# Graph layers on one core: products two steps behind the transposes, and five buffers for widened blocks

## The chip, the cores and the metric

The kernel runs on one core of a Trainium2 chip. The time is that of one launch on the device, in microseconds; the median of three runs counts.

## What is computed

Four graph blocks over 6250 nodes with 256 features, each followed by a residual and a normalisation. The second of them is three layers of one kind, so six times the kernel sums rows of neighbours over 106250 edges and multiplies the sums with 256x256 matrices:

```python
x_neigh = segment_sum(edge_w[:, None] * x[src], dst, N)         # pass 0
out = x @ w_self.T + x_neigh @ w_neigh.T                        # then row norm, residual, layernorm

z = (1.0 + eps) * h + segment_sum(h[src], dst, N)               # passes 1, 2, 3
m = relu(z @ W1 + b1) @ W2 + b2
h = relu(layernorm(m + h) * gamma + beta)

x = segment_sum(h * rsqrt(deg_out))[...] * rsqrt(deg_in) @ W_gc + feats @ W_res     # pass 4
core = top-2 of 64 experts (256 -> 512 -> 256)                  # between passes 4 and 5

out = (x - segment_sum(edge_val * x[col]) * (diag + 1)) @ weight + bias             # pass 5
```

## The kernel before, in words

The 6250 rows are 49 tiles of 128. A pass makes, tile by tile, the sum over edges in PSUM on PE, then the matrix products, the normalisation and the new rows, which go to HBM for the next pass. A tile's sum comes in one of three ways. **Sparse** tiles: POOL gathers the source rows of 128 edges with one indirect DMA (L2394), DVE makes a one-hot of their targets (picks, L3077 and L3079), PE multiplies the two (L2469, L2473, L2476); 18 such chunks make a tile. **Dense** tiles (24 of 49, in passes 1 to 4): the adjacency counts of the tile against all 49 source tiles lie in HBM as blocks of bytes, built once in pass 0; SP loads them in parts of seven blocks (`AB`, four buffers), ACT widens them to 32 bits in parts of three or four blocks (`widen`, L2944, into `WIDE`), and PE multiplies a block with the resident rows of its source tile (L2498 in passes 2 to 4, L2501 in pass 1). **Weighted** tiles (8 in pass 0, 13 in pass 5): blocks with edge weights are made on the fly from one-hots (L2523, L2563 on PE, L2909 and L2911 on ACT, L3198 on DVE).

The order is written out by hand in **steps**. A step has three gathered chunks; passes 0 to 5 have 246, 150, 150, 150, 150 and 216 such steps and a few more in which the last tiles run out (`STEPS`). In every pass each engine runs a loop over the same steps and does its own share of each, so a step is no barrier: each engine waits only for the semaphores that its instructions need. About 8.3 dense blocks belong to a step of passes 1 to 4. `SEQ` gives the step in which a tile's sum is complete: 6j+5 for sparse tiles, steps 1 and 3 of six for dense ones (so all are odd, often two apart), 2 of six for weighted ones (three from a sparse neighbour). The table `OFFSETS` says how many steps later each event of the tile is done:

- Z: the operand is made of the sum (DVE L3344, L3347, L3350; ACT L2821 in pass 0).
- T: PE transposes it into PSUM bank 2 (L2601), ACT copies it out to `TZT` (L2831).
- H (passes 1 to 3): PE multiplies with W1 (L2610), ACT takes bias and relu into `TM1` (L2838).
- L: PE makes the layer's product (L2625), from `TM1` in passes 1 to 3, from `TZT` in the others.
- A, F, Q, F2, Q2, F3, N, R: norm, residual and statistics (DVE L3376, L3378), root on ACT (L2813), scaling, new rows, their low parts. S: SP stores them. GT, G, LG: the gate of the experts in pass 4 (PE L2634, L2652 and the ranks L2642 to L2644; ACT L2861; DVE L3420 and on).
- O and X: SP loads rows for pass 4 and pass 3.

On PE a step is: dense blocks, three chunks, then the events in the order of the tiles, then building work of passes 0 and 5. On ACT it is: the widening for the next step's blocks, copies of built blocks, events, one-hots. A part of blocks is widened one step ahead of its use:

```python
return k, max(0, dense_step(b) - 1)                    # L1435, the step at which a part is widened
if e >= XA:
    act.wait_ge(s_dq, e - XA + 1)                      # in widen: part e-XA is done with
```

DVE's step is: picks for two steps ahead (which wait for the chunks of the step before, since the ring has four groups), the events, then background work: sorting edges into bins (L3082 on), one-hots of blocks (L3198), histograms (L3263 to L3266). The transposes wait for the copy of the transposes before; in passes 0 and 5, whose layer product lies in the same PSUM bank, they also wait for the finish (F) of the tile before:

```python
if k in (0, 5) and n or k == 1 and p == 0:
    pe.wait_ge(s_u, n)                                 # in transposes
```

In the eight steps after a pass's last chunk PE also multiplies the first 28 blocks of the next pass (`HEAD_PACE` = 4, 1, 1, 1, 1, 6, 7, 7 by step). The next pass's gathers wait for all new rows to be stored.

Of the kernel before, what the change touches and what calls it, by code (L numbers as in the profile page):

```python
# [5 lines left out]
N = 6250  # L6
# [34 lines left out]
def general(nc, ctx, a, out, PS):  # L41
# [1322 lines left out]
GT = WT // GC  # L1364
# [34 lines left out]
AW = max(b - a for a, b in zip(QB, QB[1:])) * P // 4  # L1399
XB = sorted({b for a, e in zip(QB, QB[1:]) for b in (a, (a + e + 1) // 2)} | {NT})  # L1400
XN = len(XB) - 1
XA = 3
XW = max(b - a for a, b in zip(XB, XB[1:])) * P
RP = 2 * D
HST = RP + 2
# [8 lines left out]
MCR = 120  # L1414
PACK_AT = [1 + 25 * i // 8 for i in range(len(SPARSE[5]))]
LASTB = {0: 26, 5: 7 + PACE}
OFFSETS = [dict(Z=1, T=2, L=3, A=4, F=5, Q=6, F2=7, N=8, R=9, S=10)] + \
    [dict(O=-1, Z=1, T=2, H=3, L=4, F=5, Q=6, F2=7, R=8, S=9)] * 2 + \
    [dict(O=-1, Z=1, T=2, H=3, L=4, X=4, F=5, Q=6, F2=7, Q2=8, F3=9, N=9, R=10, S=11)] + \
    [dict(O=-1, Z=1, T=2, L=3, F=4, GT=5, G=6, LG=7), dict(Z=1, T=2, L=3, F=4, Q=5, F2=6, N=7)]  # L1420
STEPS = [GROUPS[k] + max(9, *OFFSETS[k].values()) for k in range(PASSES)]


# [41 lines left out]
for _k in range(PASSES):  # L1465
    for _p, (_e, _t, _, _) in enumerate(SEQ[_k]):
        for _name, _o in OFFSETS[_k].items():
            EVENTS[_k].setdefault(_e + _o, []).append((_name, _p))
# [10 lines left out]
for _k in range(1, 5):  # L1479
    _at = 0  # L1480
    for _r in range(RBG):
        _stored = max(SEQ[_k - 1][PLACE[_k - 1][t]][0] for t in range(3 * _r, min(3 * _r + 3, NT))) + OFFSETS[_k - 1]["S"]
        _at = max(_at + 1, _stored + 2, (GROUPS[0] - 6 if _k == 1 else DSTEPS + 1) + _r)
# [21 lines left out]
def gnn(nc, a, out):  # L1505
# [5 lines left out]
    with ctx:  # L1511
# [40 lines left out]
        WIDE_AT = -(-PL // 8) * 8  # L1552
        BB = -(-(WIDE_AT + XA * XW) // 8) * 8
        PLANES = rounded("plane_rows", 0, PL)
        WIDE = rounded("wide_blocks", WIDE_AT, XA * XW)
        SLOTR = rounded("slot_rows", 3 * NT * D, RING * GC * HST)
# [470 lines left out]
        def events(k, g):  # L2027
            return sorted(EVENTS[k].get(g, []), key=lambda e: (e[1], OFFSETS[k][e[0]]))

# [410 lines left out]
        def _(pe):  # L2440
# [38 lines left out]
            def dense(k, found):  # L2479
                for b in found:  # L2480
# [8 lines left out]
                    if i == 0 and t % 3 == 0:  # L2489
# [5 lines left out]
                        pe.wait_ge(s_rl[r % 3], 16 * (r // 3 + 1))  # L2495
                    at_block = e % XA * XW + (t - XB[x]) * P
                    if k > 1:
# [296 lines left out]
        def _(act):  # L2794
# [139 lines left out]
            def widen(k, e):  # L2934
# [4 lines left out]
                if XB[x] == QB[q]:  # L2939
                    act.wait_ge(s_al[n % QA], 16 * (n // QA + 1))  # L2940
                if e >= XA:
                    act.wait_ge(s_dq, e - XA + 1)
                lo, w = (XB[x] - QB[q]) * P, (XB[x + 1] - XB[x]) * P
                fn(WIDE[:, e % XA * XW:e % XA * XW + w], AB[n % QA][:, lo:lo + w], ACT.Copy).then_inc(s_ax, 1)  # L2944

# [745 lines left out]
```

## Time and profile before

| | us |
|---|---|
| three runs | 5908.39, 5938.55, 5950.65 |
| median | 5938.55 |
| profiled execution | 5919.13 |
| its span, first to last instruction | 5917.4 |

Over the span PE is busy 4715.8 us (80%), DVE 3840.7 (65%), POOL 3409.4 (58%), ACT 2329.9 (39%), and TensorE's granted clock is 0.905 of full on average. By the transposes, passes 0 to 4 begin at 75, 1215, 1931, 2675 and 3382 us, pass 5 at 4982; between passes 4 and 5 lie the experts. Busy times are unions of an engine's instructions; the idle time in a row of lines is that of the engine just before the instructions of the row, with what ended it. "remote" is a semaphore whose setter the profile cannot name, "issue" no release that it shows.

### The profile page before, as it was taken

To read this page: it belongs to the slowest core of one execution; us is meant where nothing else is said; L and a number is where in the kernel's file an instruction comes from. 1 tells how busy PE (TensorE), PEld (TensorE's weight loads), DVE (VectorE), ACT (ScalarE), POOL (GpSimd) and SP (SyncE) were. 2 spreads that over 40 slices of the span, in tenths; PEclk is the share of its full clock that TensorE was granted. 3 is DMA by queue.
4 is the path that set the end of the run, shared out by engine and by line. 5 is a ranking of instruction groups with operands and counts; after the bars stand their busy time and mean duration, and the time that the engine had idled before them with its cause. 6 is when DMAs were issued, how large, how long until landed. Compare 5 with 4: busy or idle time off the path is not lost.

```text
span 5917.4 us, 84727 instructions
## 1 busy us (share of the span) xinstructions
PE 4715.8 (80%) x26215; PEld 3890.9 (66%) x26215; DVE 3840.7 (65%) x12470; ACT 2329.9 (39%) x5927; POOL 3409.4 (58%) x3425
## 2 busy tenths in 40 slices
PE   5988976678886777868888688884989857889896
PEld 3877764478885666656666477663878734777775
DVE  6788888367776777647889454447777545444443
ACT  3888875333332333324444233330333213333332
POOL 5666666566665555656666566552433263666665
PEclk8999998789998999989999799886999968999998
DMA  5333334577778666787778877663999933333333
GB/s 147 109 116 112 119 115 122 188 225 217 218 221 284 199 204 198 219 288 229 244 241 247 297 219 219 202 205 115 318 308 318 303 86 100 97 96 97 97 98 88
DMA packets 598239, 1113.22 MB, mean 188 GB/s; under 512 B 107962, under 2 KB 347320, under 8 KB 597500
## 3 DMA queue, kind: packets, MB, share of 16 engines
q0 software_dynamic: 221664, 684.44, 39.8%
q1 hardware_dynamic: 376122, 423.29, 21.8%
q8 instruction: 218, 3.57, 0.2%
q14 instruction: 235, 1.93, 0.1%
HBM read 994.01 MB, written 114.65 MB: 187 GB/s over the span
## 4 chain that ended last, share of the span: by engine, by line
PE 38%; another core or an unknown queue 9%; issue 9%; DVE 6%; ACT 2%; POOL 2%; DMA 2%; SPq 0%; ACTq 0%; DVEq 0%; POOLq 0%
PE PS L2498 11%; PE PS L2730 4%; PE PS L2625 4%; PE PS L2739 3%; PE PS L2469 3%; PE PS L2563 3%; PE PS L2476 3%; PE PS L2523 2%; POOL ring L2394 1%; PE PS L2610 1%; PE PS L2749 1%; ACT wide_blocks L2944 1%; PE PS L2601 1%; POOL ring L2423 1%
## 5 line engine op out<-in xcount | busy, mean ns | idle before, releaser
L2394 POOL DMA_INDIRECT slot_rows<-planes,REC x1800 | 1741.2, 967 | 1075.7 <-issue 468.4
L2944 ACT ACTIVATE wide_blocks<-HH 128x512 fp32r<-128x512 uint8 x1344 | 741.2, 573 | 1074.2 <-PE PS L2498 467.4
L2498 PE MATMUL PS<-plane_rows,wide_blocks 128*128 128x512 f32 x3528 | 1028.1, 434 | 122.0 <-ACT wide_blocks L2944 82.4
L2498 PEld LDWEIGHTS PS<-plane_rows,wide_blocks 128*128 128x128 f32 x3528 | 691.1, 204 | 300.4 <-ACT wide_blocks L2944 98.9
L2394 POOL DMA_INDIRECT ring<-in_x,REC x555 | 539.2, 971 | 312.9 <-issue 143.0
L2394 POOL DMA_INDIRECT ring<-table,REC x486 | 467.9, 963 | 319.1 <-issue 208.9
L2476 PE MATMUL PS<-ring,pick 128*128 128x256 f32 x2082 | 565.5, 408 | 81.6 <-DMA ring<-in_x,REC 26.9
L2476 PEld LDWEIGHTS PS<-ring,pick 128*128 128x128 f32 x2082 | 409.5, 204 | 169.7 <-issue 48.2
L2523 PE MATMUL PS<-HH 128*128 128x256 f32 (+2 forms) x1650 | 396.3, 357 | 150.4 <-issue 56.0
L2563 PE MATMUL PS<-HH 128*128 128x256 f32 x2058 | 504.3, 387 | 10.4 <-issue 10.2
L3079 DVE TENSOR_SCALAR slot_picks<-iotab,REC 128x128 fp32r<-128x128 bf16 x1800 | 411.7, 301 | 96.0 <-remote 43.9
L2909 ACT ACTIVATE HH<-iota,HH 128x128 bf16<-128x128 f32 (+1 forms) x962 | 329.3, 392 | 342.9 <-remote 197.1
L2414 POOL DMA_INDIRECT ring<-second_outputs,ring x120 | 222.2, 1852 | 411.6 <-PE PS L2720 326.8
L2469 PE MATMUL PS<-slot_rows,slot_picks 128*128 128x512 f32 x1350 | 424.6, 423 | 34.5 <-DMA slot_rows<-planes,REC 25.1
L2563 PEld LDWEIGHTS PS<-HH 128*128 128x128 f32 x2058 | 396.3, 195 | 72.7 <-issue 17.1
L2501 PE MATMUL PS<-plane_rows,wide_blocks 128*128 128x256 f32 (+1 forms) x2352 | 356.8, 303 | 78.7 <-ACT wide_blocks L2944 42.2
L2625 PE MATMUL PS<-WA,TZT 128*128 128x256 f32 x980 | 289.7, 443 | 148.8 <-ACT TZT L2831 124.5
L2523 PEld LDWEIGHTS PS<-HH 128*128 128x128 f32 (+1 forms) x1650 | 254.9, 164 | 231.6 <-issue 162.1
L2831 ACT ACTIVATE TZT<-PS 128x256 f32<-128x256 f32 (+1 forms) x294 | 132.5, 451 | 662.1 <-remote 442.7
L2501 PEld LDWEIGHTS PS<-plane_rows,wide_blocks 128*128 128x128 f32 x2352 | 318.0, 202 | 95.5 <-issue 44.3
L3077 DVE TENSOR_SCALAR pick<-iotab,REC 128x128 f32<-128x128 bf16 x1041 | 300.2, 359 | 121.2 <-remote 38.2
L3200 DVE TENSOR_SCALAR HH<-HH 128x256 f32<-128x256 f32 x338 | 127.2, 419 | 381.9 <-remote 218.7
(376 smaller groups left out, 8911.7 us busy)
## 6 DMA issues: line engine op xcount, KB each, us to landing
HH<-in_L_gnn_w SPq DMA_DIRECT2D x240, 512.0 KB
HH<-dense_blocks SPq DMA_DIRECT2D x672, 112.0 KB
plane_rows<-planes SPq DMA_DIRECT2D x64, 768.0 KB
planes<-HN SPq DMA_DIRECT2D x188, 256.0 KB
slot_rows<-planes,REC POOLq DMA_INDIRECT x1800
dense_blocks<-HH SPq DMA_DIRECT2D x24, 784.0 KB
more<-in_L_gnn_b SPq DMA_DIRECT2D x120, 128.0 KB
expert_outputs<-ring SPq DMA_DIRECT2D x120, 128.0 KB
```

Source lines behind the costliest of these rows:

```text
L2394: pool.indirect_dma_start(to, None, planes[k] if dense else tables[k], bass.IndirectOffsetOnAxis(ap=at_rows, axis=0)).then_inc(s_slot[slot ...
L2469: last = mm(bank(j % 2, RP), slot_pick(k, slot), slot_row(k, slot, 0, RP), start=c == 0, stop=c == WT - 1)
L2476: last = mm(bank(j % 2, D), slot_pick(k, slot), slot_row(k, slot, 0, D), start=c == 0, stop=c == WT - 1)
L2498: last = mm(bank(5 + n % 2, RP), WIDE[:, at_block:at_block + P], plane(0, t, RP), start=t == 0, stop=t == NT - 1)
L2501: last = mm(bank(5 + n % 2, w), WIDE[:, at_block:at_block + P], plane(m, t, w), start=t == 0 and m == 0, stop=t == NT - 1 and m == 1, skip ...
L2523: last = mm(bank(b, w, j * 2 * P), sources[slot][:, j * P:(j + 1) * P], targets[slot][:, j * 2 * P:j * 2 * P + w], start=True, stop=not ow ...
L2563: last = mm(bank(sums_bank(v), D), AW32[f % OWN][:, s % 4 * P:(s % 4 + 1) * P], x_tile(SUMMED[v][0], s), start=pos == 0 and s == sources[0 ...
L2625: last = mm(bank(layer_bank(k), D), v, wmat(m, b), start=i == 0, stop=i == len(pairs) - 1)
L2909: last = fn(to[:, j * P:(j + 1) * P], iota[:, :], ACT.Square, bias=lanes[:, 1, 2 * m + j:2 * m + j + 1], scale=-1.0)
L2944: fn(WIDE[:, e % XA * XW:e % XA * XW + w], AB[n % QA][:, lo:lo + w], ACT.Copy).then_inc(s_ax, 1)
L3077: last = v.tensor_scalar(p, iotab, lo, we, ALU.is_equal, ALU.mult)
L3079: last = v.tensor_scalar(p, iotab, lo, None, ALU.is_equal)
```

## The change

`XA`, the number of buffers for widened parts, becomes 5 (it takes 1024 more words of each partition's row, and what lies behind moves up). In `OFFSETS` H stands two steps after T in place of one, and L two steps after H (passes 1 to 3) or after T (passes 0, 4, 5) in place of one; all later events move by as much, 1 or 2 steps, and in pass 4 the gate's product is one step further behind its transposes. The extra steps at a pass's end grow by one or two.

```diff
-XA = 3
+XA = 5
...
-OFFSETS = [dict(Z=1, T=2, L=3, A=4, F=5, Q=6, F2=7, N=8, R=9, S=10)] + \
-    [dict(O=-1, Z=1, T=2, H=3, L=4, F=5, Q=6, F2=7, R=8, S=9)] * 2 + \
-    [dict(O=-1, Z=1, T=2, H=3, L=4, X=4, F=5, Q=6, F2=7, Q2=8, F3=9, N=9, R=10, S=11)] + \
-    [dict(O=-1, Z=1, T=2, L=3, F=4, GT=5, G=6, LG=7), dict(Z=1, T=2, L=3, F=4, Q=5, F2=6, N=7)]
+OFFSETS = [dict(Z=1, T=2, L=4, A=5, F=6, Q=7, F2=8, N=9, R=10, S=11)] + \
+    [dict(O=-1, Z=1, T=2, H=4, L=6, F=7, Q=8, F2=9, R=10, S=11)] * 2 + \
+    [dict(O=-1, Z=1, T=2, H=4, L=6, X=6, F=7, Q=8, F2=9, Q2=10, F3=11, N=11, R=12, S=13)] + \
+    [dict(O=-1, Z=1, T=2, L=4, F=5, GT=6, G=8, LG=9), dict(Z=1, T=2, L=4, F=5, Q=6, F2=7, N=8)]
```

PE in the middle of pass 2, before. L2601 are a tile's transposes, L2610 and L2625 its two products, L2498 dense blocks, L2469 chunks, L2580 a histogram:

```order
L2625 MATMUL PS<-WA,TM 128x256 x2
L2601 MATMUL PS<-ident,TZ 128x128 x2
L2498 MATMUL PS<-plane_rows,wide_blocks 128x512 x9
L2469 MATMUL PS<-slot_rows,slot_picks 128x512 x3
L2610 MATMUL PS<-TZT,WA 128x128 x4
L2498 MATMUL PS<-plane_rows,wide_blocks 128x512 x8
L2469 MATMUL PS<-slot_rows,slot_picks 128x512 x3
L2580 MATMUL PS<-HH 128x49 x18
L2625 MATMUL PS<-WA,TM 128x256 x2
```

and after, from a tile's transposes to its first product (its second product is the next L2625, six rows further on):

```order
L2601 MATMUL PS<-ident,TZ 128x128 x2
L2498 MATMUL PS<-plane_rows,wide_blocks 128x512 x9
L2469 MATMUL PS<-slot_rows,slot_picks 128x512 x3
L2498 MATMUL PS<-plane_rows,wide_blocks 128x512 x8
L2469 MATMUL PS<-slot_rows,slot_picks 128x512 x3
L2580 MATMUL PS<-HH 128x49 x18
L2625 MATMUL PS<-WA,TM 128x256 x2
L2610 MATMUL PS<-TZT,WA 128x128 x4
```

A tile's first product stood one step of blocks and chunks behind its transposes. Now two steps lie between, and the first product shares its step with the second product of the tile before.

ACT at the same place, before. L2831 copies transposes, L2838 is the relu, L2944 widens, L2813 is a root:

```order
L2838 ACTIVATE TM<-PS,B1C 128x128 x2
L2944 ACTIVATE wide_blocks<-HH 128x512
L2944 ACTIVATE wide_blocks<-HH 128x384
L2831 ACTIVATE TZT<-PS 128x256
L2944 ACTIVATE wide_blocks<-HH 128x512
L2944 ACTIVATE wide_blocks<-HH 128x384
L2944 ACTIVATE wide_blocks<-HH 128x512
L2838 ACTIVATE TM<-PS,B1C 128x128 x2
L2944 ACTIVATE wide_blocks<-HH 128x384
```

and after:

```order
L2838 ACTIVATE TM<-PS,B1C 128x128 x2
L2831 ACTIVATE TZT<-PS 128x256
L2944 ACTIVATE wide_blocks<-HH 128x512
L2944 ACTIVATE wide_blocks<-HH 128x384
L2944 ACTIVATE wide_blocks<-HH 128x512
L2944 ACTIVATE wide_blocks<-HH 128x384
L2944 ACTIVATE wide_blocks<-HH 128x512
L2838 ACTIVATE TM<-PS,B1C 128x128 x2
L2944 ACTIVATE wide_blocks<-HH 128x384
```

The relu now stands just ahead of the next copy of transposes. The widening stands behind the copy as before.

DVE in pass 0, at the sixth tile, whose follower is a weighted tile, before. L3374 to L3322 are the tile's finish, L3077 picks, L3138 and L3140 sorting, L3198 one-hots:

```order
L3077 TENSOR_SCALAR pick<-iotab,REC 128x128 x3
L3374 TENSOR_SCALAR SM<-SM 128x1
L3375 RECIPROCAL SM<-SM 128x1
L3376 SCALAR_TENSOR_TENSOR TU<-PS,SM,HH 128x256
L3320 BN_STATS ST<-TU 128x6
L3321 BN_AGGR MV<-ST 128x2
L3322 TENSOR_SCALAR SM<-MV 128x1
L3138 TENSOR_TENSOR HH<-LANES,PS 128x2304
L3198 TENSOR_SCALAR HH<-HH 128x256 x4
L3077 TENSOR_SCALAR more<-iotab,REC 128x128 x3
L3140 CAST PS<-HH 128x90
L3141 TENSOR_TENSOR HH<-iotab,PS 128x468
```

and after:

```order
L3077 TENSOR_SCALAR pick<-iotab,REC 128x128 x3
L3138 TENSOR_TENSOR HH<-LANES,PS 128x2304
L3198 TENSOR_SCALAR HH<-HH 128x256 x4
L3077 TENSOR_SCALAR more<-iotab,REC 128x128 x3
L3374 TENSOR_SCALAR SM<-SM 128x1
L3375 RECIPROCAL SM<-SM 128x1
L3376 SCALAR_TENSOR_TENSOR TU<-PS,SM,HH 128x256
L3320 BN_STATS ST<-TU 128x6
L3321 BN_AGGR MV<-ST 128x2
L3322 TENSOR_SCALAR SM<-MV 128x1
L3140 CAST PS<-HH 128x90
L3141 TENSOR_TENSOR HH<-iotab,PS 128x468
```

The finish has moved behind L3138, the one-hots and the picks of the step after.

## Rows read from the trace of the kernel before

**Rows 1.** Stretches of passes 0 to 4: us, busy of PE, PEld, DVE, ACT, POOL; PEclk; DMA.

```profile
60.00:1170.00 1110.00, 890.18 (x4436) 716.36 (x4437) 847.58 (x2876) 776.95 (x2106) 694.93 (x714) 0.91 0.40 122
1170.00:1885.00 715.00, 581.22 (x4178) 548.02 (x4178) 513.29 (x1620) 237.43 (x582) 441.85 (x452) 0.90 0.77 235
1885.00:2628.00 743.00, 572.27 (x3197) 444.33 (x3196) 492.64 (x1284) 231.29 (x532) 430.92 (x452) 0.91 0.73 220
2628.00:3330.00 702.00, 559.37 (x2554) 432.78 (x2553) 563.36 (x1810) 292.06 (x726) 443.62 (x451) 0.91 0.81 253
3330.00:4090.00 760.00, 600.88 (x2655) 478.95 (x2654) 376.15 (x1622) 230.71 (x439) 428.88 (x452) 0.87 0.69 206
```

**Rows 2.** Lines of POOL, whole span: POOL's gathers of passes 1 to 4.

```profile
L2394 POOL DMA_INDIRECT slot_rows<-planes,REC x1800 | 1741.2, 967 | 1075.7 <-issue 468.4 <-remote 293.9 <-PE PS L2469 248.9
```

**Rows 3.** Lines of PE, pass 1: busy us, mean ns | idle before us, releasers.

```profile
L2501 PE MATMUL PS<-plane_rows,wide_blocks 128*128 128x256 f32 (+1 forms) x2334 | 353.8, 303 | 78.7 <-ACT wide_blocks L2944 42.2 <-issue 29.8 <-DVE plane_rows L3463 5.4
L2625 PE MATMUL PS<-WA,TM 128*128 128x256 f32 x192 | 57.3, 426 | 24.3 <-ACT TM L2838 13.8 <-issue 10.4
```

**Rows 4.** Lines of PE, pass 2.

```profile
L2498 PE MATMUL PS<-plane_rows,wide_blocks 128*128 128x512 f32 x1176 | 340.7, 434 | 27.1 <-ACT wide_blocks L2944 21.6 <-issue 5.5
L2625 PE MATMUL PS<-WA,TM 128*128 128x256 f32 x196 | 60.8, 437 | 20.8 <-issue 16.9 <-ACT TM L2838 4.0
L2610 PE MATMUL PS<-TZT,WA 128*128 128x128 f32 x395 | 57.5, 291 | 35.7 <-ACT TZT L2831 31.3 <-issue 4.3
```

**Rows 5.** Lines of PE, pass 3.

```profile
L2498 PE MATMUL PS<-plane_rows,wide_blocks 128*128 128x512 f32 x1176 | 341.4, 430 | 54.4 <-ACT wide_blocks L2944 36.6 <-issue 17.5
L2625 PE MATMUL PS<-WA,TM 128*128 128x256 f32 x196 | 59.0, 428 | 32.5 <-ACT TM L2838 23.2 <-issue 9.2
```

**Rows 6.** Lines of PE, pass 4.

```profile
L2498 PE MATMUL PS<-plane_rows,wide_blocks 128*128 128x512 f32 x1170 | 342.9, 437 | 40.5 <-ACT wide_blocks L2944 24.2 <-issue 16.1
L2625 PE MATMUL PS<-WA,TZT 128*128 128x256 f32 x392 | 122.6, 468 | 72.5 <-ACT TZT L2831 72.3 <-issue 0.2
```

**Rows 7.** Waits of ACT: total us, times, longest us.

```profile
ACT wide_blocks L2944 <- PE PS L2498: 467.4, 354, 7.1
ACT TZT L2831 <- remote: 442.7, 85, 18.7
```

**Rows 8.** Timeline, pass 4: start us, us, engine, line [idle before <-releaser].

```profile
3755.57 0.42 PE L2601 MATMUL PS<-ident,TZ 128*128 128x128 f32 x2
...
3763.51 0.62 DVE L3420 TENSOR_TENSOR HH<-HH,PS 128x64 f32<-128x64 bf16 x4 [7.25 <-remote]
3763.57 0.60 ACT L2831 ACTIVATE TZT<-PS 128x512 f32<-128x512 f32 x1 [8.85 <-remote]
...
3764.22 3.78 PE L2625 MATMUL PS<-WA,TZT 128*128 128x256 f32 x8 [5.44 <-ACT TZT L2831]
```

**Rows 9.** Timeline, end of pass 2, PE alone.

```profile
2629.28 1.13 PE L2625 MATMUL PS<-WA,TM 128*128 128x256 f32 x4 [0.48 <-ACT TM L2838]
2630.06 6.88 PE L2498 MATMUL PS<-plane_rows,wide_blocks 128*128 128x512 f32 x28
```

**Rows 10.** Pass 0: PE's line of the product, then a timeline of one place.

```profile
L2625 PE MATMUL PS<-WA,TZT 128*128 128x256 f32 x392 | 106.4, 420 | 22.8 <-ACT TZT L2831 11.4 <-issue 11.3
...
308.06 0.48 DVE L3376 SCALAR_TENSOR_TENSOR TU<-PS,SM,HH 128x256 f32<-128x256 f32 x1
...
308.69 0.41 PE L2601 MATMUL PS<-ident,TZ 128*128 128x128 f32 x2 [0.65 <-issue]
...
309.33 2.54 DVE L3138 TENSOR_TENSOR HH<-LANES,PS 128x2304 bf16<-128x2304 bf16 x1
...
311.79 0.87 DVE L3198 TENSOR_SCALAR HH<-HH 128x256 bf16<-128x256 bf16 x4
...
312.57 0.85 DVE L3077 TENSOR_SCALAR pick<-iotab,REC 128x128 f32<-128x128 bf16 x3
```

**Rows 11.** Lines of PE, pass 5.

```profile
L2625 PE MATMUL PS<-WA,TZT 128*128 128x256 f32 x196 | 60.7, 438 | 53.5 <-ACT TZT L2831 40.7 <-issue 12.8
```


## The prediction

> **What bounds the kernel now.** I read the stretches first. Passes 1 to 4 take 715, 743, 702 and 760 us. No engine is full in any of them: PE has 559 to 601 us busy, DVE 376 to 563, ACT 231 to 292, POOL 429 to 444 [rows 1]. POOL adds 468.4 us of its own spacing between 1800 gathers to 1741.2 us of work [rows 2], so it needs about 552 us of a pass. The passes are bound by waits between engines that all run in a fixed order.
>
> The second view is the PE's lines of each pass with the idle time ahead of them. Ahead of the products over widened blocks (L2498, L2501) PE idles 78.7, 27.1, 54.4 and 40.5 us, mostly until ACT has widened a block: 200.7 us [rows 3 to 6]. Ahead of the second product on the relu'd operand (L2625 on TM) it idles 24.3, 20.8 and 32.5 us, together 77.6; ahead of the first product (L2610) 35.7 in pass 2, where it matters; ahead of pass 4's product on transposes (L2625 on TZT) 72.5 [rows 3 to 6]. These 386 us are copies on ACT that come too late.
>
> The third view, the waits, says why ACT is late with blocks: its widening waits 467.4 us, in 354 places, for PE to give a buffer of the three back, and its copy of transposes waits 442.7 us for a signal [rows 7]. The timeline of one place in pass 4 shows the second kind: the transposes start at 3755.57, PE goes on with a step of 11 products until 3758.8, ACT's copy starts only at 3763.57, and PE sits 5.44 us until 3764.22. DVE, which waits for the gate's products just ahead of those transposes, is let go at the same moment, after 7.25 us [rows 8]. PE's matmuls are drawn as ended long before ACT is let go. So a signal of PE can be 7 us late, and what counts is how much work PE has that needs nothing behind that signal.
>
> The Trainium skill (Perfetto Trace Analysis, "Summary: the profiler window per engine type") says that a matmul's end in a profile is estimated and the signal's way is not in it; the trace agrees, and shows far more than a propagation here.
>
> **Part one, five buffers.** A part of 3 or 4 blocks is widened one step before it is used, and today waits for the part three before it; with five, for the part five before it. PE has then four parts, 14 blocks or 1.7 steps of some 4.5 us, between the signal and the need, in place of two parts. Such lateness as rows 8 show is 7 us at worst, so waits of this kind should nearly all go. Not all of the 200.7 us is of this kind: part has no releaser in the view. I take 0.7 of it, 140 us. The bounds are 0 and 200.7.
>
> **Part two, products two steps behind.** The first product moves from one to two steps after the transposes, the second from one to two steps after the first, and every later event by as much. One thing does not move: ACT's copy of the transposes, and behind it, on ACT, the widening for the step after next. The order of ACT shows blocks queued right behind the copies. So where a late signal of the transposes holds ACT, PE runs one step, skips what was the first product, and stops at the next block instead. The 35.7 us ahead of L2610 I therefore count as not gained (bounds: 35.7 gained; 20 lost, since ACT has relu, copy and a widening, 1.6 us, ahead of PE's next work where it had one copy).
>
> The wait for the relu is another matter. Tiles end on odd steps alone; first product and transposes now share odd steps, and even steps hold neither. ACT has one place per two steps to be held in place of two. I take half of 77.6 us, 39 us (bounds 0 and 77.6). In pass 4 the product, 122.6 us in 49 tiles or 2.5 us each [rows 6], now stands between the gate's small products and the transposes, and the signal that is late is that of the gate's products: the transposes' share of the lateness shrinks by that. Half of 72.5 us, 36 us (bounds 0 and 72.5).
>
> The Trainium skill (TensorE: Matmul & The Clock Gate, "Architectural detail: the array is 16× 32×32, not 1× 128×128") has ACT and DVE as strict first-in first-out queues. That rule speaks against this part. Taken alone it would give part two nothing in the passes with blocks; rival one below is that case.
>
> Together 215 us of PE's waits. What comes late next: DVE (563 us busy of 702 in pass 3, with its chained small steps between) and POOL's 552 us and the idle time between passes. I keep 0.55 of it, a choice between 0 and 1 nearer the middle because no engine is busy for more than 81% of any of these passes [rows 1]: 118 us.
>
> **Where it costs.** At the end of passes 0 to 3 the last tile's products stand among the 28 blocks with which the next pass begins: the first now has one block more before it, the second seven more. 28 blocks take 6.88 us, so 0.246 each: eight are 2.0 us, less waits of PE that they fill, such as the 0.48 us ahead of the product now [rows 9]. Some 1 us at each of four ends: 4 us.
>
> Pass 0: transposes and the layer's product share a PSUM bank, so the next tile's transposes wait for DVE's finishing of this one. A weighted tile ends 3 steps from its neighbours. There the transposes already follow DVE's finish by 0.15 us (308.06 with 0.48 us, then 308.69). Now DVE's finish stands behind one more piece of the background work: 2.54 us, 0.87 us and the next picks 0.85 us, 4.3 us later [rows 10]. Eight such places are 34 us of PE, the eight other neighbours about 1 us each. DVE, with 848 of 1110 us busy [rows 1], sets the pace there and mostly does not wait for PE, so I count 15 us (bounds 0 and 42). Ahead of the product itself 22.8 us of waits may shrink [rows 10]; that is inside this 15.
>
> Pass 5 has the same rule and 26 such places, but no sorting on DVE. PE waits 53.5 us ahead of L2625 [rows 11]. Builds behind the same ACT queue take over half of it, and the later finish some 17 us: a gain of 10 us (bounds 40 gained, 30 lost).
>
> **Sum.** -118 +4 +15 -10 = -109 us. The profiled execution took 5919.1 us (span 5917.4), so 5810; the median of three is 5938.55, 19 us above it, and a change is compared in medians: 5830.
>
> **Rivals.**
> One: the stall only moves. ACT is held by the same late signals, and PE stops at the next block. For it: rows 8, and that ACT's order is unchanged. Against: 467.4 us of ACT's wait is for buffers. Then part one keeps 40 us and the rest cancels against 19 us of costs: 5915.
>
> Two: the full release. The waits go and nothing takes their place; all 215 us come through, with the same 9 us of costs: 5733. For it: POOL's 552 us. Against: DVE's load in passes 1 to 3.
>
> Three: slower. The finish that comes a DVE step later turns passes 0 and 5 into a hand-over in every weighted neighbourhood: the transposes wait, ACT's copies and one-hots queue behind them, and DVE then lacks its inputs. The price is a DVE step, 4.3 us, at all 16 + 26 places, 180 us, less 110 us in the blocks' passes: 6010. It decides when PE, behind at such a place, also starves DVE's picks two steps on; PE is at 890 of 1110 us in pass 0, so it isn't far. Against: DVE has as much work left in the step as PE has to catch up.
>
> Four: that the change doesn't do what it says. The order shows it does, on all three engines.
>
> **Chances.** Forecast 0.49 (its own range 5770 to 5885), rival one 0.21, rival two 0.15, rival three 0.15. The range 5740 to 5960 takes in most of rivals one and two and leaves rival three out. A measurement of this kernel can tell about 1% (59 us) from no change. Faster by over 1%: nearly all of the forecast and all of rival two, 0.62. Within 1%: rival one and the forecast's upper edge, 0.23. Slower: 0.15.
>
> **What would show it.** ACT's wait for PE L2498 ahead of its widening should fall from 467.4 us to under 200, and PE's idle time ahead of the blocks from 200.7 to about 60 to 100. The waits ahead of L2625 on TM should halve; those ahead of L2610 should vanish from that line, with blocks in their place just after odd steps. Passes 1 to 4 should each lose 15 to 40 us. In pass 0, PE's idle time ahead of L2601 at the weighted neighbourhoods should rise from 0.65 us in rows 10 to some 4. I am wrong if the idle time ahead of the blocks doesn't fall, or if passes 0 or 5 grow by over 30 us.

## The result

| eleven runs each, side by side | median, us | lowest to highest |
|---|---|---|
| before | 5942.17 | 5908.39 to 5952.92 |
| changed | 5960.73 | 5952.2 to 5972.2 |

The ratio is 1.0036, with a 95% interval of 1.0019 to 1.0053: the change costs 0.4%. The forecast was 5830 us, and the time lies 0.7 us above the range of 5740 to 5960; it moved the other way than forecast. The two profiled executions took 5919.13 and 5952.2 us (spans 5917.4 and 5950.5), 33 us apart. Measured from a pass's first transposes to its last, the lengths are:

| us | pass 0 | 1 | 2 | 3 | 4 | 5 | the rest of the span |
|---|---|---|---|---|---|---|---|
| before | 1091.7 | 668.9 | 696.3 | 653.7 | 700.6 | 921.6 | 1184.6 |
| changed | 1135.1 | 667.7 | 711.7 | 656.1 | 666.2 | 924.4 | 1189.3 |
| difference | +43.4 | -1.2 | +15.3 | +2.4 | -34.4 | +2.8 | +4.7 |

So pass 0 lost 43 us, and passes 1 to 4, where 118 us were to be gained, gained 18: pass 4 alone gained 34, and passes 1 to 3 together lost 17. Each of these lengths is from one execution of each kernel. The changed kernel's stretches between those transposes, passes 0 to 4, with the columns of [rows 1]:

```profile
75.19:1210.28 1135.09, 881.25 (x4384) 713.29 (x4382) 836.72 (x2836) 776.55 (x2098) 685.61 (x705) 0.90 0.39 117
1258.55:1926.24 667.69, 561.95 (x4002) 525.94 (x4001) 496.08 (x1555) 215.71 (x557) 419.11 (x427) 0.91 0.76 229
1972.76:2684.44 711.68, 558.06 (x3081) 435.98 (x3077) 478.55 (x1243) 199.98 (x505) 409.42 (x427) 0.89 0.71 215
2731.00:3387.14 656.14, 536.18 (x2451) 423.24 (x2450) 546.16 (x1747) 265.70 (x694) 415.24 (x427) 0.90 0.80 250
3440.39:4106.55 666.16, 548.43 (x2539) 442.01 (x2538) 351.37 (x1515) 199.53 (x407) 405.67 (x428) 0.91 0.72 215
```

The waits that the change was to cure did go from where they stood. PE's lines of passes 1 to 4, in this order, in stretches that answer to those of [rows 3 to 6]:

```profile
L2501 PE MATMUL PS<-plane_rows,wide_blocks 128*128 128x256 f32 (+1 forms) x2332 | 354.8, 302 | 74.8 <-issue 53.8 <-ACT wide_blocks L2944 14.4 <-DVE plane_rows L3463 5.6
L2625 PE MATMUL PS<-WA,TM 128*128 128x256 f32 x192 | 57.3, 425 | 0.9 <-issue 0.8
...
L2498 PE MATMUL PS<-plane_rows,wide_blocks 128*128 128x512 f32 x1177 | 340.2, 432 | 82.9 <-ACT wide_blocks L2944 74.5 <-issue 8.4
L2610 PE MATMUL PS<-TZT,WA 128*128 128x128 f32 x397 | 61.3, 304 | 1.9 <-ACT TZT L2831 1.9
...
L2498 PE MATMUL PS<-plane_rows,wide_blocks 128*128 128x512 f32 x1176 | 341.5, 431 | 65.1 <-ACT wide_blocks L2944 34.7 <-issue 29.8
L2625 PE MATMUL PS<-WA,TM 128*128 128x256 f32 x196 | 55.1, 406 | 7.6 <-ACT TM L2838 6.0 <-issue 1.7
...
L2498 PE MATMUL PS<-plane_rows,wide_blocks 128*128 128x512 f32 x1169 | 335.8, 429 | 89.3 <-ACT wide_blocks L2944 50.8 <-issue 38.5
L2625 PE MATMUL PS<-WA,TZT 128*128 128x256 f32 x392 | 101.5, 405 | 0.7 <-ACT TZT L2831 0.7
```

The second product (L2625) waited 77.6 us in three passes and 72.5 in pass 4; now it waits 11 and 0.7. But ahead of the blocks (L2501, L2498) PE idles 312 us where it had been 200.7. The waits of ACT tell why, beside [rows 7]; the row of DVE is pass 0's and is taken up further down. First the relu's wait in the kernel before, then the changed kernel's rows:

```profile
ACT TM L2838 <- remote: 139.9, 27, 12.1
```

```profile
ACT TM L2838 <- remote: 551.4, 85, 16.0
ACT TZT L2831 <- remote: 412.7, 77, 22.8
...
DVE SM L3374 <- ACT SM L2809: 138.9, 31, 11.8
...
ACT wide_blocks L2944 <- PE PS L2498: 170.5, 114, 6.7
```

The widening waits much less for a buffer (170.5 us by this row, 467.4 before); it now stands behind the relu and the copy, which wait for a signal of PE. Taking all rows of a line together, whatever they name, ACT's waits ahead of the widening fell from 1068 to 456 us, those ahead of the relu rose from 210 to 724 and those ahead of the copy of transposes from 661 to 751: 612 us went, 604 came. A place in pass 2, in the changed kernel's timeline:

```profile
2492.78 2.11 PE L2498 MATMUL PS<-plane_rows,wide_blocks 128*128 128x512 f32 x8
...
2494.73 0.86 PE L2469 MATMUL PS<-slot_rows,slot_picks 128*128 128x512 f32 x3
...
2501.39 0.62 ACT L2838 ACTIVATE TM<-PS,B1C 128x128 f32<-128x128 f32 x2 [12.91 <-remote]
...
2501.91 1.97 ACT L2944 ACTIVATE wide_blocks<-HH 128x384 fp32r<-128x384 uint8 x4
...
2502.48 1.22 PE L2498 MATMUL PS<-plane_rows,wide_blocks 128*128 128x512 f32 x2 [6.90 <-ACT wide_blocks L2944]
```

PE's first product is over by 2493.0, it goes on through eight blocks and three chunks, and then waits 6.90 us for a block. ACT widens that block straight after the relu, and the relu had been waiting 12.91 us, the last 8.4 of them after the product was drawn as ended. It is the picture of [rows 8], with the block in the product's place. (Whether the block's bytes and buffer were there much earlier than the relu, the trace doesn't show; when ACT reached it they were.)

### The profile page after: what moved, and what is told of

It is laid out like the page before. It is cut to its first block, busy times and chain, and to the rows that moved or that the text cites. A ratio compares the mean times of both kernels' runs of the same rounds, so it can differ in the third digit from the quotient of the medians.

```text
span 5950.5 us, 84745 instructions
## 1 busy us (share of the span) xinstructions
PE 4745.3 (80%) x26215; PEld 3920.6 (66%) x26215; DVE 3846.3 (65%) x12470; ACT 2277.2 (38%) x5927; POOL 3399.4 (57%) x3425
## 3 DMA queue, kind: packets, MB, share of 16 engines
q1 hardware_dynamic: 376122, 423.29, 21.5%
## 4 chain that ended last, share of the span: by engine, by line
PE 34%; DVE 10%; issue 9%; another core or an unknown queue 8%; DMA 2%; ACT 2%; POOL 1%; SPq 0%; ACTq 0%; DVEq 0%; POOLq 0%
PE PS L2498 8%; PE PS L2563 4%; PE PS L2730 4%; PE PS L2739 4%; PE PS L2476 3%; PE PS L2625 3%; PE PS L2469 3%; PE PS L2523 2%; DVE slot_picks L3079 1%; ACT wide_blocks L2944 1%; PE PS L2749 1%; PE PS L2601 1%; POOL ring L2423 1%; DVE HH L3266 1%
## 5 line engine op out<-in xcount | busy, mean ns | idle before, releaser
L2498 PE MATMUL PS<-plane_rows,wide_blocks 128*128 128x512 f32 x3528 | 1020.7, 431 | 237.3 <-ACT wide_blocks L2944 160.0
L2498 PEld LDWEIGHTS PS<-plane_rows,wide_blocks 128*128 128x128 f32 x3528 | 696.5, 205 | 432.6 <-ACT wide_blocks L2944 182.5
L2944 ACT ACTIVATE wide_blocks<-HH 128x512 fp32r<-128x512 uint8 x1344 | 690.0, 571 | 457.1 <-PE PS L2498 170.5
L2469 PE MATMUL PS<-slot_rows,slot_picks 128*128 128x512 f32 x1350 | 436.3, 430 | 66.3 <-DMA slot_rows<-planes,REC 42.8
L2831 ACT ACTIVATE TZT<-PS 128x256 f32<-128x256 f32 (+1 forms) x294 | 133.8, 455 | 752.9 <-remote 412.7
L2501 PE MATMUL PS<-plane_rows,wide_blocks 128*128 128x256 f32 (+1 forms) x2352 | 357.9, 302 | 74.8 <-issue 53.8
L2501 PEld LDWEIGHTS PS<-plane_rows,wide_blocks 128*128 128x128 f32 x2352 | 322.3, 205 | 90.5 <-issue 68.8
L2469 PEld LDWEIGHTS PS<-slot_rows,slot_picks 128*128 128x128 f32 x1350 | 276.9, 206 | 153.3 <-issue 61.9
L2838 ACT ACTIVATE TM<-PS,B1C 128x128 f32<-128x128 f32 x294 | 92.0, 364 | 724.2 <-remote 551.4
```

What stands on the lines that cost most here:

```text
L2469: last = mm(bank(j % 2, RP), slot_pick(k, slot), slot_row(k, slot, 0, RP), start=c == 0, stop=c == WT - 1)
L2498: last = mm(bank(5 + n % 2, RP), WIDE[:, at_block:at_block + P], plane(0, t, RP), start=t == 0, stop=t == NT - 1)
L2501: last = mm(bank(5 + n % 2, w), WIDE[:, at_block:at_block + P], plane(m, t, w), start=t == 0 and m == 0, stop=t == NT - 1 and m == 1, skip ...
```

## Two kinds of chip

The runs below fell on two kinds of chip, which nothing in the program chooses. On most, the kernel before takes 5237 to 5246 us, 12% less than in the runs above. The thirteenth and fourteenth run were on one like the first, at 5875 us. Ratios are always to the kernel before on the same chip. Each chip was used at one time only, so whether the kind belongs to the chip or to a state it was in is not shown; "kind of chip" below means no more than that.

The fifth run is the kernel before itself on the faster chip.

> The kernel before, for a profile of it on the chip that took 5243 us for it. Theory 'prompt signals' (this chip lets ACT and DVE go as soon as PE's matmuls are drawn as ended, the chip of the prediction did not): PE's idle time in passes 1 to 4 is some 280 us against 596 us in rows 3 to 6's execution, and hardly any signal of PE comes over 2 us after its matmul's recorded end. Rival 'clock': the idle time is as in the first profile, and the 700 us lie in fewer stretches at half clock.

Measured: 5236.93 us. Its stretches of passes 0, 2 and 4 and its waits of ACT:

```profile
76.14:1070.05 993.91, 844.66 (x4384) 687.82 (x4382) 827.53 (x2838) 772.85 (x2099) 692.00 (x705) 0.95 0.44 134
...
1715.43:2286.88 571.45, 511.83 (x3080) 405.58 (x3076) 476.77 (x1245) 228.59 (x505) 410.12 (x430) 0.96 0.85 266
...
2988.63:3546.55 557.92, 517.16 (x2539) 419.93 (x2538) 352.37 (x1531) 222.35 (x407) 406.63 (x427) 0.97 0.83 257
```

```profile
ACT wide_blocks L2944 <- PE PS L2498: 527.9, 737, 12.8
ACT TZT L2831 <- PE PS L2601: 519.4, 243, 12.2
...
PE PS L2498 <- ACT wide_blocks L2944: 12.9, 4, 5.1
...
PE PS L2625 <- ACT TZT L2831: 4.6, 11, 0.7
```

ACT's waits for PE now name it ("remote" is gone), and PE waits 12.9 us for ACT's blocks of passes 2 to 4, where it had waited 82.4. ACT itself still waits long, 714 us ahead of the widening against 1068 and 519 ahead of the copy against 661, but this costs PE little. Of the recorded updates of the semaphore that PE's transposes raise, 105 of 251 in the first profile come over 2 us after the recorded end of the transposes before them, and here one of 295, the last of the trace. (Six passes of 49 tiles raise it 294 times; in the first profile some of these have no record of their own.) DVE, ACT and POOL are as fast on the one as on the other (POOL's work in pass 2 is 406 and 410 us). So the first chip's signals of PE are late, and this one's are prompt. Whether a late signal is slow on its way or its matmul ends later than it is drawn, the trace can't tell apart; what follows needs only that the waiting engine is let go late. In passes 1 to 4 PE's idle time is 247 us here, against 537 there, both between transposes; PE's busy time is smaller too (pass 2: 512 against 542 us), at a granted clock of 0.96 against 0.92. The expectation held for the signals and the idle time; its rival has a share: of the 419 us by which passes 1 to 4 are shorter here, 290 are PE's idle time and 129 its busy time.

## The change in parts, on a chip with prompt signals

The buffers alone:

```diff
-XA = 3
+XA = 5
```

> Five buffers, every offset as before. Theory 'moved' (ACT is held by late signals of PE, and PE stops at whatever it needs from ACT next): ACT's wait for PE L2498 ahead of the widening falls from 467 us to under 200, but PE's idle time moves to L2610, L2625 and to blocks behind the relu and the copy of transposes; the idle time of passes 1 to 4 together falls by 20 to 50 us of 596, the time is 5900 to 5930. Rival 'buffers cure, offsets spoil': the 165 us of idle time that ended with a buffer given back are gained, passes 1 to 4 are 100 to 150 us shorter, 5790 to 5840. Rival 'clock': the idle time falls but the granted clock falls with it, and the time stays within 5 us of 5942.

Measured: 5233.15 us, ratio 0.9976 (0.9967 to 0.9985): 10 us. On this kind of chip PE hardly waits for blocks, so there was little to move or to cure, and the expectation, made for the other kind, stays untested.

The offsets alone (all of `OFFSETS` new, `XA = 3`):

> All new offsets, three buffers as before. Theory 'moved': the waits for the relu and the copy go from L2625 and L2610, the waits for buffers stay at L2498 and L2501 (some 165 us or more), pass 0 has its whole loss of 43 us: 5970 to 6010. Rival 'offsets help': the copies' waits of 180 us fall to half, and with pass 0's loss the time is 5900 to 5930.

Measured: 5342.62 us, ratio 1.0188 (1.0175 to 1.0201). Pass 0 takes 1072.4 us, against 993.9 in the fifth run; no other pass is over 16 us longer. The ratio is above that of the whole change on this kind of chip (1.0136, below), clear of both intervals: beside the new offsets the five buffers are worth 0.5%, by themselves 0.2%. What the 0.5% are made of was not looked at.

The change in passes 1 to 4 alone:

```diff
-OFFSETS = [dict(Z=1, T=2, L=4, A=5, F=6, Q=7, F2=8, N=9, R=10, S=11)] + \
+OFFSETS = [dict(Z=1, T=2, L=3, A=4, F=5, Q=6, F2=7, N=8, R=9, S=10)] + \
...
-dict(Z=1, T=2, L=4, F=5, Q=6, F2=7, N=8)]
+dict(Z=1, T=2, L=3, F=4, Q=5, F2=6, N=7)]
```

> The changed kernel, with the offsets of before in passes 0 and 5. Theory 'finish' (the 43 us that pass 0 lost come of its own offsets): pass 0 is back at 1092 us between its first and last transposes, passes 1 to 4 stay as in the changed kernel, 5910 to 5925. Rival (pass 0's loss is a chance of one execution, or comes from the head of pass 1 and its buffers): pass 0 keeps 20 us or more of the loss, and the time stays above 5940.

Measured: 5244.41 us, ratio 1.0003 (0.9994 to 1.0011), with pass 0 at 999.5 us. The whole change on such a chip:

> The changed kernel beside the experiments, on their chip if it is to be had. Theory 'finish': its passes 0 and 5 are those of the second experiment (pass 0 75 us longer than before), its passes 1 to 4 those of the third (no change): 1.013 to 1.016 times before. Rival: the five buffers take part of pass 0's loss away, since the first 28 blocks of pass 1 are widened at its end: under 1.008. On a chip with late signals of PE, as that of the prediction, 1.0036 as before.

Measured: 5318.43 us, ratio 1.0136 (1.0121 to 1.0152). Pass 0 is 77 us longer than before, pass 5 3 us shorter, and passes 1 to 4 together level (+4.7, +11.2, -9.8, -5.5). On this kind of chip the loss is pass 0's. ACT's waits move here as they did on the first chip (ahead of the widening 714 to 209 us, of the relu 162 to 548, of the copy 519 to 657), but here ACT is back in time: PE idles 13 us ahead of the blocks of passes 1 to 4, against 15 in the kernel before. (The expectation's rival, that the buffers take part of pass 0's loss away, fails: it is 77 us with them and 78 without.)

## Why pass 0 lost

First the fifth run's timeline (before), then the sixth's (changed), at the same weighted tile:

```profile
368.86 0.48 DVE L3376 SCALAR_TENSOR_TENSOR TU<-PS,SM,HH 128x256 f32<-128x256 f32 x1
...
369.50 0.41 PE L2601 MATMUL PS<-ident,TZ 128*128 128x128 f32 x2 [2.87 <-DVE TU L3376]
...
374.24 1.89 PE L2625 MATMUL PS<-WA,TZT 128*128 128x256 f32 x8
...
379.23 0.20 ACT L2809 ACTIVATE SM<-SM 128x1 f32<-128x1 f32 x1
...
380.47 0.15 DVE L3374 TENSOR_SCALAR SM<-SM 128x1 f32<-128x1 f32 x1
```

```profile
393.66 0.48 DVE L3376 SCALAR_TENSOR_TENSOR TU<-PS,SM,HH 128x256 f32<-128x256 f32 x1
...
394.29 0.66 PE L2601 MATMUL PS<-ident,TZ 128*128 128x128 f32 x2 [9.73 <-DVE TU L3376]
...
404.92 1.89 PE L2625 MATMUL PS<-WA,TZT 128*128 128x256 f32 x8
...
410.20 0.20 ACT L2809 ACTIVATE SM<-SM 128x1 f32<-128x1 f32 x1
...
410.54 0.15 DVE L3374 TENSOR_SCALAR SM<-SM 128x1 f32<-128x1 f32 x1 [4.55 <-ACT SM L2809]
```

Finish, transposes, product, root and finish are a loop through all three engines, since transposes and product share a bank. Two things happen in it. The transposes wait 9.73 us for the finish in place of 2.87: DVE does it a step later. And from the transposes to the product it is now 10.6 us in place of 4.7, so the root comes late, and DVE, which had not waited at this place, stands still for 4.55. The first wait stands in nine places of pass 0, which has eight weighted tiles, the second in 29 (rows below). Two runs take them apart. The seventh leaves the product late and puts the finish back:

```diff
-OFFSETS = [dict(Z=1, T=2, L=4, A=5, F=6, Q=7, F2=8, N=9, R=10, S=11)] + \
+OFFSETS = [dict(Z=1, T=2, L=4, A=5, F=5, Q=7, F2=8, N=9, R=10, S=11)] + \
```

> The changed kernel with one number changed: in pass 0 DVE's finish F stands five steps after the sum, as before, though the product L stays two steps behind the transposes. Theory 'finish' (what pass 0 lost is that PE's transposes of a weighted neighbour wait for a finish that DVE does a step later than PE does the transposes): pass 0 is within 12 us of that of before and the time is 60 us or more under the changed kernel's. Rival 'product' (the loss is L's own move, which fills the step of the neighbour's transposes): nothing is gained, pass 0 stays 40 to 75 us longer than before.

Measured: 5298.01 us, ratio 1.0106 (1.0089 to 1.0123), pass 0 1050.4 us: 20 us under the changed kernel. Neither side was right: the finish is neither the whole loss nor nothing. The seventh is not a clean half of the change, though: the root (A) is late with the product, and the finish that needs it (F) now stands in the same step, where both kernels have a step between. The eighth is the third experiment's kernel with the finish late and product and root as before:

```diff
-OFFSETS = [dict(Z=1, T=2, L=3, A=4, F=5, Q=6, F2=7, N=8, R=9, S=10)] + \
+OFFSETS = [dict(Z=1, T=2, L=3, A=4, F=6, Q=7, F2=8, N=9, R=10, S=11)] + \
```

> The third experiment's kernel, with pass 0's product L and root of the norm where they were, and DVE's finish F and all behind it one step later, as the change has them. Theory 'finish': the whole loss of pass 0 is there (70 to 80 us where PE's signals are prompt, 40 to 50 where they are late), though L has not moved. Rival 'product': pass 0 is within 12 us of before's.

Measured: 5278.7 us, ratio 1.0063 (1.0049 to 1.0077), pass 0 1026.1 us. Again neither side was right. The waits of pass 0, in the fifth, sixth, seventh and eighth run:

```profile
DVE SM L3374 <- ACT SM L2809: 37.5, 15, 7.2
...
PE PS L2601 <- DVE TU L3376: 25.8, 9, 4.8
```

```profile
DVE SM L3374 <- ACT SM L2809: 105.7, 29, 6.8
...
PE PS L2601 <- DVE TU L3376: 80.1, 9, 11.5
```

```profile
DVE SM L3374 <- ACT SM L2809: 141.0, 33, 11.1
...
PE PS L2601 <- DVE TU L3376: 45.4, 9, 7.5
```

```profile
PE PS L2601 <- DVE TU L3376: 44.9, 8, 8.1
...
DVE SM L3374 <- ACT SM L2809: 3.9, 3, 2.0
```

The late finish alone makes pass 0 32 us longer than before, and PE's waits for it grow from 25.8 to 44.9 us. The late product, with the finish where it was, makes it 56 us longer, and DVE's waits for the root grow from 37.5 to 141.0 us, a part of which is the missing step between root and finish. Both together cost 77, so beside the late finish the late product costs 45: it is the larger part either way. DVE has 828 of 994 us busy in this pass, and its idle time follows the loss: 166 us before, 189, 218 and 234 in the eighth, seventh and sixth run, so 23, 51 and 67 us more where the pass is 32, 56 and 77 us longer. The single rows don't add up that way: in the seventh run 103 us more stand at the root, while other waits of DVE shrink.

## Where the gain of passes 1 to 4 went

The theory: ACT's order is copy or relu first, widening behind it; a late signal holds both, and the change only gives PE another thing to wait for. Its test is to move nothing but ACT's place for these copies, one step later. The kernel is the third experiment's, and these copies have offsets of their own, `TC`, `HC` and `GTC`, each a step behind PE's:

```diff
-    [dict(O=-1, Z=1, T=2, H=4, L=6, F=7, Q=8, F2=9, R=10, S=11)] * 2 + \
+    [dict(O=-1, Z=1, T=2, TC=3, H=4, HC=5, L=6, F=7, Q=8, F2=9, R=10, S=11)] * 2 + \
...
-                        if name == "T":
+                        if name == ("TC" if "TC" in OFFSETS[k] else "T"):
                             copy_transposes(k, p)
-                        if name == "H":
+                        if name == "HC":
                             hidden(k, p)
...
-                        if name == "GT":
+                        if name == "GTC":
                             gate_copy(p)
```

> As e3, and in passes 1 to 4 ACT's copy of the transposes, its relu and its copy of the gate's transposes each stand one step later in ACT's order (PE and DVE unchanged), so that a widening is never queued behind a signal that PE gave in the same step. Theory 'moved': PE's idle time ahead of blocks that ended with a copy, a relu or a gate copy (16+64+35+39+35 = about 190 us, with 25 us behind L2831 in passes 1 to 3) falls to under 60, and the time is 80 to 140 us below e3: 5780 to 5840. Rival 'clock': the idle time falls as much, but stretches at half clock grow, and the time is within 30 us of e3. Rival 'DVE or POOL next': the idle time comes back ahead of chunks (L2469, L2473) and transposes, at the same clock, and the time is within 30 us of e3.

Measured: 5242.13 us, ratio 1.0000 (0.9991 to 1.0008). It fell on a chip with prompt signals, where the waits to be cured hardly exist, and says nothing on the theory.

So lateness was made by hand. In four kernels ACT waits, before each of these copies in passes 1 to 4, besides for PE's chunks of the step after the one in which PE gave the signal. The ninth is this in the kernel before:

```diff
+                        if k in DENSE_PASSES and name in ("T", "H", "GT") and g + 1 < GROUPS[k]:
+                            act.wait_ge(s_prod, group(k, g + 1) + 1)
```

> The kernel before, and in passes 1 to 4 ACT's copy of transposes, its relu and its copy of the gate's transposes wait besides for PE's chunks of the following step: a stand-in, on a chip with prompt signals, for signals of PE that come a step (some 3.5 us) late. Theory 'moved': PE, which needs each copy right behind those chunks, stands still for one copy or relu each time, some 0.85 us at 98 places in each of four passes: 300 to 340 us above before, with the idle time at L2610 and L2625. If the chip's signals are late in themselves, less is added, since a part of the wait is there already.

Measured: 5407.06 us, ratio 1.0308 (1.0289 to 1.0328): +166 us, half of what was expected. The tenth is the ninth with five buffers:

> As the ninth, with five buffers. Theory 'moved' (buffers do nothing against late transposes): within 15 us of the ninth. Rival (with ACT held, three buffers become the limit and five lift it): 50 us or more under the ninth.

Measured: 5390.31 us, 1.0284 (1.0267 to 1.0301), 17 us under the ninth, of which they gave 10 without any delay: the buffers do next to nothing against late copies. The eleventh is the change in passes 1 to 4 with the delay:

> The same delay in the third experiment's kernel (the change in passes 1 to 4 alone). Theory 'moved': the idle time leaves L2610 and L2625 and stands at the blocks (L2498, L2501), since the widening is queued behind the copy and the relu; ACT is held once in two steps, for a relu, a copy and a widening, 1.7 us at 49 places a pass: 280 to 340 us above the third's, within 60 us of the ninth. Rival 'two steps cure it' (what the change is built for): under 60 us above the third's, that is 250 us or more below the ninth.

Measured: 5365.83 us, 1.0238 (1.0221 to 1.0256): 121 us above the same kernel without delay, under half of what was expected, and 41 under the ninth. The twelfth is the late copies with the delay (`g` for `g + 1`, since ACT does them a step later):

> The same delay in the fourth experiment's kernel, in which ACT does copies and relu a step later. Theory 'moved': no widening is queued behind a late signal any more, and PE has a whole step for the copy: under 40 us above the fourth's, 240 us or more below the eleventh. Rival 'clock or another engine next': the idle time goes elsewhere, and the time is within 100 us of the eleventh.

Measured: 5240.77 us, 1.0004 (0.9994 to 1.0014), 125 us below the eleventh. The delay costs nothing that can be measured. PE's lines of pass 2 in the ninth, eleventh and twelfth run:

```profile
L2610 PE MATMUL PS<-TZT,WA 128*128 128x128 f32 x384 | 57.4, 294 | 22.7 <-ACT TZT L2831 22.7
...
L2625 PE MATMUL PS<-WA,TM 128*128 128x256 f32 x192 | 54.3, 405 | 18.4 <-ACT TM L2838 18.4
```

```profile
L2498 PE MATMUL PS<-plane_rows,wide_blocks 128*128 128x512 f32 x1104 | 300.2, 407 | 59.0 <-ACT wide_blocks L2944 59.0
...
L2610 PE MATMUL PS<-TZT,WA 128*128 128x128 f32 x384 | 54.1, 286 | 0.0
...
L2625 PE MATMUL PS<-WA,TM 128*128 128x256 f32 x192 | 53.4, 401 | 0.0
```

```profile
L2498 PE MATMUL PS<-plane_rows,wide_blocks 128*128 128x512 f32 x1104 | 293.5, 410 | 0.0
```

That is the changed kernel's picture made to order: 41 us leave the two products and 59 stand ahead of the blocks (0.0 in the ninth run). Over passes 1 to 4, between transposes, PE idles 358 us in the ninth run and 354 in the eleventh: the change moved the idle time and took none of it away. The 48 us by which the eleventh's PE is busy for less (2059 against 2106) come with a higher granted clock (pass 2: 0.99 against 0.95). In the twelfth, where the widening is no longer behind a fresh signal, the idle time is 226. The same test with three buffers, `XA = 3`, came next:

> The twelfth experiment's kernel with three buffers in place of five: late copies, the stand-in delay of one step. Theory 'place': what cures is that no widening and no product stands right behind a late signal; three buffers do: within 20 us of the twelfth (5241). Rival 'room': held for a step, ACT reaches a widening later and needs the room of five buffers to be ahead again; with three PE waits for blocks, 60 us or more above it.

This run fell on a chip with late signals (before: 5875.21 us). Measured: 5882.12 us, ratio 1.0010 (0.9994 to 1.0025). The expectation compared it with the twelfth run, on another kind of chip, so it stays untested. Beside it, on the same chip, ran the late copies with five buffers and without delay:

> The fourth experiment's kernel once more, for the case that a chip with late signals runs it. There (before about 5940 us) the theory says that PE's idle time behind copies, relus and gate copies goes, and the time is 2% or more below before, 5700 to 5820; rival 'clock': it comes back as half-clock stretches and the time is 5900 or more. On a chip with prompt signals the ratio is again within 0.1% of 1.

Measured: 5848.52 us, ratio 0.9957 (0.9939 to 0.9975): faster than before, but by 27 us, where the theory had said 2% (118 us) or more. It is 34 us under the thirteenth, which differs in two things, the delay and the three buffers. Pass 4 takes 656.5 us, and passes 1 to 4 together 2650 in this execution, against 2720 and 2702 in the first two profiles, which may be another chip's. Its lines of passes 1 and 2 and one of its waits:

```profile
L2501 PE MATMUL PS<-plane_rows,wide_blocks 128*128 128x256 f32 (+1 forms) x2196 | 328.3, 297 | 63.0 <-issue 62.2
...
L2498 PE MATMUL PS<-plane_rows,wide_blocks 128*128 128x512 f32 x1104 | 302.0, 416 | 15.5 <-issue 8.3 <-ACT wide_blocks L2944 6.8
...
L2580 PE MATMUL PS<-HH 128*128 128x49 bf16 x871 | 34.8, 194 | 106.8 <-DVE HH L3266 84.8 <-issue 22.1
```

```profile
ACT wide_blocks L2944 <- remote: 292.7, 108, 9.7
```

The blocks are cured in part. Between the same transposes PE idles ahead of them 63.0, 15.5, 21.5 and 40.1 us in passes 1 to 4, together 140; it was 282 in the changed kernel (64.1, 80.3, 59.2, 78.1) and 168 in the kernel before. Pass 1's 63 us did not move, and the view names no releaser for them. Elsewhere other waits come: in pass 2 the histograms, whose one-hots DVE makes, wait 106.8 us, where they had waited 55.5 in the changed kernel and 69.9 before. Over passes 1 to 4 PE still idles 475 us, against 497 and 537. My reading is that signals of all kinds are late on such a chip, and that the next order with a step to spare and no more, DVE's, takes the copies' place; no run moved DVE's order to test it.

Three kernels were run once more, in the hope of a chip with late signals; it was one with prompt signals. They repeat the first, third and sixth run:

> The first experiment's kernel, for a chip with late signals (before at 5850 us or more). Theory 'moved': the 165 us of idle time that ended with a buffer given back go, and most comes back at the relu and the copy (L2610, L2625): 0.994 to 1.000 times before. Rival 'buffers cure': 0.975 to 0.985. On a chip with prompt signals 0.998 as before.

Measured: 5229.89 us, 0.9980 (0.9970 to 0.9989).

> The third experiment's kernel, for a chip with late signals. Theory 'moved, with some gain': 0.993 to 0.998 times before, passes 1 to 4 together 15 to 40 us shorter, and the late copies' kernel (0.9957 in the fourteenth run) is not more than 0.5% ahead of it. Rival 'late copies are the cure there too': it is 1.000 or more, and the late copies' 0.4% are all of their own. On a chip with prompt signals 1.000.

Measured: 5244.09 us, 1.0007 (0.9998 to 1.0016).

> The changed kernel beside the two. On a chip with late signals 1.002 to 1.006 times before, with pass 0 35 to 50 us longer than in the other two kernels; that difference to the sixteenth run is the price of pass 0 there, 0.6 to 0.9%. On a chip with prompt signals 1.012 to 1.016.

Measured: 5316.76 us, 1.0142 (1.0124 to 1.0161). All three agree with what was expected for prompt signals; the late kind stays untested for them.

## Why the prediction was wrong

**Part one** was right in what it saw and wrong in what it was worth. ACT's wait for PE's blocks fell from 467.4 to 170.5 us, "under 200" as forecast. But "I take 0.7 of it, 140 us" counted a wait as gained because its releaser would be gone. ACT then ran into the next late signal, in front of the same widening. PE's idle time ahead of blocks was to fall to 60 to 100 us and rose to 312. That is the two parts together; what the buffers alone do on such a chip no run shows.

**Part two** named the mechanism and priced it against itself. "So where a late signal of the transposes holds ACT, PE runs one step, skips what was the first product, and stops at the next block instead" is what the changed kernel's timeline shows; it was applied to the 35.7 us of the copy and not to the 77.6 us of the relu, to pass 4 or to part one. The Trainium skill (TensorE: Matmul & The Clock Gate, "Architectural detail: the array is 16× 32×32, not 1× 128×128") has ACT and DVE as strict first-in first-out queues; by that the same holds for each of them, and the traces agree (12.91 us at the relu, 6.90 at the block behind it). Rival one was this case, at 0.21; its 5915 us were still 46 too low, 28 of them pass 0's. Adding the four lines of [rows 3 to 6] and their counterparts, 386 us of waits became 326: 60 us, of the 215 counted on. Between transposes all of PE's idle time in passes 1 to 4 fell by 40 us (537 to 497). Its busy time rose by 36 us in passes 1 to 3 and fell by 14 in pass 4, mostly as the granted clock went (pass 2: 0.92 to 0.89, pass 4: 0.89 to 0.91). 40 less 22 is the 18 us.

**"I keep 0.55 of it ... 118 us"** is therefore the step that failed most: 18 us were measured, from one execution of each. Of the 215 us under the factor 60 went; the sum took waits as gone that only changed their place. Pass 4 gained 34 us, where I had 36 for its product before the factor; that the two agree is luck, since its blocks wait 49 us longer and its PE is busy 14 us less.

**Pass 0**: "so I count 15 us (bounds 0 and 42)". It was 43 on the first chip and 77 on the other. The wait of the transposes was foreseen (between the pass's first and last transposes PE's idle time ahead of L2601 on TZ went from 12.9 to 53.6 us), and so was its size before the "so" (34 us; 32 in the eighth run, on the other kind of chip). The sentence after it, that DVE "mostly does not wait for PE", was wrong: the product's own step later makes DVE wait for the root, the larger part (45 to 56 us there), and no term had it. On the chip of the forecast this wait grew from 56.8 to 138.9 us, and DVE's idle time in the pass by 41 us. Rival three, at 0.15, has DVE starve, but of its picks, and in both passes; pass 5, where the finish moved from four steps to five and no further than it stood in pass 0 before, lost 2.8 us on the first chip and gained 3.3 on the other. Both signs that I had named for being wrong came: the idle time ahead of the blocks didn't fall, and pass 0 grew by over 30 us.

**The tails and pass 5**: forecast +4 and -10, measured +4.7 for all that lies outside the passes and +2.8 for pass 5.

Not settled: what the change in passes 1 to 4, or either of its parts, gives in medians on a chip with late signals. None of them ran there by itself; 18 us is a difference of two profiles. So it is open, too, how much of the fourteenth run's 27 us is the place of the copies. Whether three buffers do for the late copies is open as well.

## What to carry to other kernels

Ahead of moving a product further from its operand, look at what stands behind the copy of that operand on the copying engine: a consumer that is moved away from a late signal gains nothing if its own next input queues behind the same wait. Give the added step to the copy too: with a delay of one step made by hand this took 125 us off (twelfth run against the eleventh). On a chip whose signals really are late it gave 27 us against the kernel before, so don't expect the whole of a wait back. And where two operations share a bank through a third engine, draw the loop before adding a step to it. In pass 0, where DVE in the loop is busy for 828 of 994 us, the steps cost 77 us; pass 5 has such a loop too, with DVE busy for 430 of 794 us, and lost nothing (3 us more on one chip, 3 less on the other).

## What was not expected of the hardware

The same program takes 5243 us on one chip and 5942 or 5875 on others. POOL, DVE and ACT work equally fast on them; what differs is that PE's signals come up to some 8 us after the recorded end of its matmuls on the latter (7 us in [rows 8], 8.4 at the relu in pass 2 above), and that the granted clock is lower (0.905 against 0.936 for the kernel before). What makes the signals late, and whether it stays with a chip, no run here shows. In pass 0, on the chip with prompt signals, the granted clock fell with the change, from 0.95 to 0.92, while PE's idle time in the pass rose from 149 to 214 us and its busy time from 845 to 857. That the one caused the other is not shown.
